# Graph attention on one Trainium2 core: q kept as three bf16 parts, spread over edges with bf16 one-hots

## The chip, the cores and the metric

The kernel runs on one NeuronCore of a Trainium2 chip. The metric is the device time of one execution in microseconds (us). The kernel before has a median of 6509.19 us over 3 runs (6508.78 to 6512.75).

## The reference

A graph network over 3125 nodes and 100000 edges (sorted by destination). Four transformer layers with 8 heads of 16 come first, then one message-passing layer with a 64-wide message:

```python
def _transformer_conv(h, src, dst, ...):
    q = (h @ Wq.T + bq)[dst]; k = (h @ Wk.T + bk)[src]; v = (h @ Wv.T + bv)[src]   # 8 heads x 16
    alpha = jnp.sum(q * k, axis=-1) / sqrt(D_HEAD)
    ex = jnp.exp(alpha - segment_max(alpha, dst)[dst])
    a = ex / (segment_sum(ex, dst)[dst] + 1e-16)
    out = segment_sum(a[:, :, None] * v, dst)
    x_r = h @ Ws.T + bs
    beta = sigmoid(concat([out, x_r, out - x_r]) @ Wbeta.T)
    return beta * x_r + (1 - beta) * out
# L0: h = gelu(x @ Wi); 4 layers of h = layer_norm(conv(h) + h); h = ffn(h) + h; then h @ Wo
# L1: msg = silu([x[src], x[dst], rbf(dist)] @ mw1 + mb1) @ mw2; mean over dst; update MLP
```

## The kernel before, in words

Nodes lie in 25 blocks (NB) of 128 rows. Edges lie in tiles of 128, one tile per partition column; two tiles share one node block, and 16 tiles (CH) make a chunk. There are 52 chunks per layer. Each layer has two kinds of stage.

**Node stage.** DVE mixes and normalizes five blocks at a time (L1044 to L1082), PE and ACT do the feed-forward part, and then the projections of the next layer follow (L666 on PE, L995 to L1004 on DVE): for each of 5 groups of 5 blocks PE makes a 128x256 product (q and the skip term `x_r` side by side) and a 128x264 product (k and v), DVE adds the biases and writes them to `qs` and `kvst`, and SP writes `kvst` to the table `kv_table` in HBM (L297). PE waits for these evictions by the semaphore `a_ev`, two banks deep. After the last group DVE clears `f_out` and `acc` (L1006, L1007).

**Edge stage.** POOL issues one indirect DMA per tile (L352): it gathers 128 rows of `kv_table` by the indices in `idx` into `slots`, a ring of 4 chunks. It starts when the table is written (`tab_out`), `acc` is cleared (`acc_zero`) and SP has loaded `idx` (L280), and goes on as slots come free (`slot_free`, set by PE at L561). For every group of 4 tiles, DVE compares `iota` with the destinations to make float32 one-hots `oh` (L847), PE turns them (L536), ACT copies the turned ones from PSUM to `ohT` (L377), and PE multiplies `ohT` by the block's rows of `qs` (L545): that product spreads q over edges. DVE multiplies it with the gathered keys (L865) and sums over heads (L871). The scores are turned at L569, scans along edges follow (L887 to L926), then exp on ACT, the weighting of v (L945), the sums over edges on PE with `oh` as weights (L559), and the addition to `acc` (L855). The work on chunk g is interleaved with the front of chunk g+1 in an order written out by hand (`attend_step` on PE, ACT and DVE). The message layer has the same form: `src_table` in place of `kv_table`, one further product with the distance basis (L549), an addition (L962) and silu (L442) in place of the attention.

All operands of these products are float32. In the trace a float32 product is two LDWEIGHTS and two MATMUL records.

## Time and profile before

| | |
|---|---|
| median of 3 runs | 6509.19 us |
| span of the profiled execution | 8606.0 us; no time beside the span is recorded for it |
| PE / PEld / DVE / ACT / POOL busy | 4926.9 / 4250.3 / 4108.2 / 1473.0 / 4188.6 us |
| mean granted TensorE clock | 0.699 of full speed |
| edge stages of the 4 attention layers (POOL's first gather to the first node instruction) | 233 to 1779, 1926 to 3487, 3639 to 5194, 5346 to 6907 us |
| edge stage of the message layer | 7108 to 8457 us |

The profiled execution is 2097 us longer than the median of the runs, so its waits are not simply those of a run that isn't profiled; durations of single instructions and waits have to be read apart. PE is TensorE's matmul stream, PEld its weight loads, DVE VectorE, ACT ScalarE, POOL GpSimd, SP SyncE.

### The profile page before, as it was taken

How to read it: one execution, taken by the hardware profiler on the slowest of the kernel's cores; microseconds unless marked ns; L12 is line 12 of the kernel's file. 1: busy time of each engine (PE TensorE's matmuls, PEld its weight loads, DVE VectorE, ACT ScalarE, POOL GpSimd, SP SyncE). 2: the span in 40 equal slices, each digit the busy share in tenths (PEclk: the TensorE clock that was granted, in tenths of full speed). 3: DMA queues.
4: the chain of work that ended last, by engine and by line, in shares of the span. 5: the costliest groups of instructions: out<-in, count | busy, mean ns of one | idle time of the engine just before them, and what ended most of it. 6: DMA issues, size and time to landing. Idle time of an engine off the chain costs nothing.

```text
span 8606.0 us, 101311 instructions
## 1 busy us (share of the span) xinstructions
PE 4926.9 (57%) x27346; PEld 4250.3 (49%) x27347; DVE 4108.2 (48%) x10183; ACT 1473.0 (17%) x3017; POOL 4188.6 (49%) x4185
## 2 busy tenths in 40 slices
PE   2465555664565555646556566456555664666664
PEld 1355454553454445535545455445455544565664
DVE  4455555564555555645555555455555552222224
ACT  1011111120111111211111112011111132333332
POOL 0555555506555555055555541555555406666660
PEclk9666666686666666866666668666666677887876
DMA  3322222313222223132222231222222201111111
GB/s 54 89 75 78 72 73 72 74 31 85 73 71 72 75 75 71 32 80 73 74 74 76 75 65 39 79 74 75 75 74 72 61 9 48 47 47 48 46 47 9
DMA packets 278744, 545.85 MB, mean 63 GB/s; under 512 B 128939, under 2 KB 155947, under 8 KB 278652
## 3 DMA queue, kind: packets, MB, share of 16 engines
q0 software_dynamic: 187040, 506.01, 23.1%
q1 hardware_dynamic: 84540, 31.89, 1.8%
q10 hardware_dynamic: 7072, 6.82, 0.2%
q8 instruction: 46, 0.75, 0.0%
q14 instruction: 46, 0.38, 0.0%
HBM read 525.19 MB, written 17.11 MB: 63 GB/s over the span
## 4 chain that ended last, share of the span: by engine, by line
another core or an unknown queue 43%; PE 27%; issue 15%; DVE 9%; ACT 3%; DVEq 1%; ACTq 1%; DMA 0%; SPq 0%; POOL 0%; POOLq 0%
PE bank L545 8%; PE bank L536 5%; PE bank L559 3%; PE bank L549 2%; DVE acc L855 1%; PE bank L697 1%; PE bank L689 1%; DVE oh L847 1%; PE bank L601 1%; PE bank L581 1%; PE bank L519 1%; DVE slots L962 1%; PE bank L527 1%; PE bank L668 1%
## 5 line engine op out<-in xcount | busy, mean ns | idle before, releaser
L352 POOL DMA_INDIRECT slots<-kv_table,idx x3328 | 3343.6, 1005 | 3434.2 <-PE bank L559 1621.0
L545 PE MATMUL bank<-qs,ohT 128*128 x8320 | 1766.8, 363 | 903.3 <-ACT ohT L377 438.9
L545 PEld LDWEIGHTS bank<-qs,ohT 128*128 128x128 f32 x8320 | 1550.0, 269 | 1021.8 <-issue 1002.9
L559 PE MATMUL bank<-slots,oh 128*128 128x136 f32 (+1 forms) x8320 | 1234.1, 299 | 167.2 <-issue 105.1
L559 PEld LDWEIGHTS bank<-slots,oh 128*128 128x128 f32 x8320 | 1133.0, 208 | 225.1 <-issue 127.5
L352 POOL DMA_INDIRECT slots<-src_table,idx x832 | 824.8, 991 | 735.4 <-issue 501.5
L855 DVE TENSOR_TENSOR acc<-acc,bank 128x136 f32 (+1 forms) x2080 | 605.2, 291 | 1022.5 <-remote 572.5
L536 PE MATMUL bank<-ident,oh 128*128 128x128 f32 x4160 | 1008.2, 390 | 108.3 <-DVE oh L847 64.2
L377 ACT COPY ohT<-bank 128x512 f32<-128x512 f32 x1040 | 601.7, 583 | 2055.9 <-remote 1167.0
L865 DVE TENSOR_TENSOR slots<-slots,bank 128x512 f32<-128x512 f32 x832 | 567.8, 682 | 630.9 <-remote 515.8
L536 PEld LDWEIGHTS bank<-ident,oh 128*128 128x128 f32 x4160 | 748.0, 210 | 202.6 <-issue 199.2
L847 DVE TENSOR_TENSOR oh<-iota,rel_e 128x1024 f32<-128x1024 f32 x520 | 630.7, 1214 | 0.5 <-issue 0.2
L945 DVE TENSOR_TENSOR slots<-slots,bank 128x544 f32<-128x544 f32 x832 | 542.2, 714 | 129.8 <-remote 115.7
L924 DVE TENSOR_TENSOR_SCAN fwd<-resets,icol,bank 128x128 f32<-128x128 f32 (+1 forms) x208 | 99.8, 480 | 1041.3 <-ACT icol L394 840.6
L871 DVE TENSOR_REDUCE alpha<-slots 128x32 f32<-128x512 f32 x832 | 566.5, 681 | 0.9
L581 PE MATMUL bank<-ident,fwd 128*1 128x128 f32 x208 | 66.3, 319 | 656.4 <-DVE bwd L889 308.0
L601 PE MATMUL bank<-ident,ex 128*128 128x128 f32 x208 | 94.8, 456 | 577.2 <-ACT ex L402 446.1
L962 DVE TENSOR_TENSOR slots<-slots,bank 128x512 f32<-128x512 f32 x208 | 141.4, 685 | 566.0 <-remote 333.4
L385 ACT COPY f_in<-bank 1x256 f32<-1x256 f32 x208 | 75.3, 362 | 1934.7 <-remote 1281.6
L588 PE MATMUL bank<-ones,c_row 1*128 1x1 f32 x416 | 119.5, 354 | 480.6 <-DVE c_row L914 257.4
L549 PE MATMUL bank<-resets 128*128 128x128 f32 x1664 | 370.1, 308 | 14.1 <-issue 13.9
L588 PEld LDWEIGHTS bank<-ones,c_row 1*128 1x128 f32 x416 | 101.8, 302 | 559.2 <-DVE c_row L914 305.2
(217 smaller groups left out, 4440.2 us busy)
## 6 DMA issues: line engine op xcount, KB each, us to landing
slots<-kv_table,idx POOLq DMA_INDIRECT x3328
slots<-src_table,idx POOLq DMA_INDIRECT x832
kv_table<-slots SPq DMA_DIRECT2D x20, 660.0 KB, 3.4
resets<-flat_len ACTq DMA_DIRECT2D x52, 128.0 KB
idx<-src_e SPq DMA_DIRECT2D x260, 8.0 KB
w<-in_w SPq DMA_DIRECT2D x8, 256.0 KB, 3.0
resets<-flat_rst SPq DMA_DIRECT2D x8, 208.0 KB, 10.6
slots<-flat_rst SPq DMA_DIRECT2D x8, 208.0 KB, 9.9
```

What stands on the lines that cost most here:

```text
L352: pool.indirect_dma_start(slots[:, k, t, 0:width], None, table, bass.IndirectOffsetOnAxis(ap=idx[:, k, t:t + 1], axis=0))\
L377: act.copy(ohT[:, j % 2, :, :].rearrange("p a b -> p (a b)"), bank[j % 2][:, :]).then_inc(oh_copied, 1)
L536: mm = pe.transpose(bank[j % 2][:, t * P:(t + 1) * P], oh[:, k % 2, j * G + t, :], ident[:, :])
L545: mm = pe.matmul(o, ohT[:, j % 2, t, :], qs[:, blocks[(j * G + t) // 2], 0:HID], start=True, stop=basis is None)
L549: mm = pe.matmul(o, rbf[:, k % 2, half, :], m_1c[:, q, :], start=False, stop=True)
L559: mm = pe.matmul(bank[6 + j % 2][:, o:o + width], oh[:, k % 2, t, :], slots[:, k, t, HID:HID + width], start=(t % 2 == 0), stop=(t % 2 == 1))
L847: dve.tensor_tensor(oh[:, k % 2, half * H:(half + 1) * H, :], bc(iota[:, :], H), bcl(rel_e[:, bass.ds(c * CH + half * H, H)], P), ALU.is_e ...
L855: dve.tensor_tensor(a_s, a_s, bank[6 + s // 2 % 2][:, o:o + width], ALU.add).then_inc(acc_done, 1)
L865: dve.tensor_tensor(keys, keys, bank[2 + j % 2][:, :].rearrange("p (t k) -> p t k", t=G), ALU.mult).then_inc(spread_used, 1)
L871: dve.tensor_reduce(alpha[:, :, j * G:(j + 1) * G].rearrange("p h t -> p t h"), slots[:, k, j * G:(j + 1) * G, 0:HID].rearrange("p t (h d) ...
L945: dve.tensor_tensor(vals, vals, bcl(exs[:, j * G:(j + 1) * G, :], VW), ALU.mult).then_inc(w_done, 1)
L962: dve.tensor_tensor(slots[:, k, j * G:(j + 1) * G, HID:2 * HID], slots[:, k, j * G:(j + 1) * G, 0:HID], bank[2 + j % 2][:, :].rearrange("p ...
```

## The change

`qs` (q and x_r side by side, float32) is replaced by `xr` (float32) and `q3`, which holds q as three bf16 tensors: q rounded to bf16, the rest rounded to bf16, and the rest of that. `ohT` becomes bf16 (ACT's copy L377 writes it so). The spreading product L545 becomes three products with the same `ohT` that add up in PSUM. DVE makes the parts in a new function after each group of five blocks, with four instructions that wait for each other. PSUM evictions of q and x_r are two instructions in place of one, so `a_ev` counts 3 per block in the attention layers.

```diff
-        qs = sb("qs", [P, NB, QS])
+        xr = sb("xr", [P, NB, HID])
+        q3 = sb("q3", [P, NB, 3, HID], BF16)
-        ohT = sb("ohT", [P, 2, G, P])
+        ohT = sb("ohT", [P, 2, G, P], BF16)
+        qf, qr = o_all[:, 0:BW, :], o_all[:, BW:2 * BW, :]
...
-                    mm = pe.matmul(o, ohT[:, j % 2, t, :], qs[:, blocks[(j * G + t) // 2], 0:HID],
-                                   start=True, stop=basis is None)
+                    for part in range(3):
+                        mm = pe.matmul(o, ohT[:, j % 2, t, :], q3[:, blocks[(j * G + t) // 2], part, :],
+                                       start=part == 0, stop=basis is None and part == 2)
...
+            def split_rows(i, nth, evicted):
+
+                def part(m):
+                    return q3[:, bass.ds(i * BW, BW), m, :]
+
+                dve.wait_ge(a_ev, evicted)
+                dve.tensor_copy(part(0), qf).then_inc(q_parts, 1)
+                dve.wait_ge(q_parts, START + 4 * nth + 1)
+                dve.tensor_tensor(qr, qf, part(0), ALU.subtract).then_inc(q_parts, 1)
+                dve.wait_ge(q_parts, START + 4 * nth + 2)
+                dve.tensor_copy(part(1), qr).then_inc(q_parts, 1)
+                dve.wait_ge(q_parts, START + 4 * nth + 3)
+                dve.tensor_tensor(part(2), qr, part(1), ALU.subtract).then_inc(q_parts, 1)
+                dve.wait_ge(q_parts, START + 4 * nth + 4)
...
-                        dve.tensor_tensor(qs[:, i * BW + b, :], bank[2 + b % 2][:, 0:QS], vec_qskv[:, 0:QS],
+                        dve.tensor_tensor(qf[:, b, :], bank[2 + b % 2][:, 0:HID], vec_qskv[:, 0:HID],
+                                          ALU.add).then_inc(a_ev, 1)
+                        dve.tensor_tensor(xr[:, bass.ds(i * BW + b, 1), :].rearrange("p a k -> p (a k)"),
+                                          bank[2 + b % 2][:, HID:QS], vec_qskv[:, HID:QS],
                                           ALU.add).then_inc(a_ev, 1)
...
+                    split_rows(i, ga, START + 3 * BW * (ga + 1))
```

In the message layer q's place is taken by the destination's part of the message input (L1110), which goes to `qf` and through `split_rows` in the same way.

## Rows read from the trace of the kernel before

**Rows 1.** Groups of instructions: POOL's gathers (busy us, mean ns, idle before and its releasers).
```profile
L352 POOL DMA_INDIRECT slots<-kv_table,idx x3328 | 3343.6, 1005 | 3434.2 <-PE bank L559 1621.0 <-issue 969.3 <-DMA idx<-src_e 789.3
L352 POOL DMA_INDIRECT slots<-src_table,idx x832 | 824.8, 991 | 735.4 <-issue 501.5 <-remote 164.2 <-DMA idx<-src_e 51.6
```

**Rows 2.** Timeline: first gathers of three layers, the first layer's end, the last gather.
```profile
233.34 0.94 POOL L352 DMA_INDIRECT slots<-kv_table,idx  x1 [167.31 <-DMA idx<-src_e]
...
1721.38 0.94 POOL L352 DMA_INDIRECT slots<-kv_table,idx  x1 [0.30 <-issue]
...
1779.15 0.29 DVE L1027 TENSOR_TENSOR slots<-vec 128x128 f32<-128x128 f32 x1
...
1925.92 0.94 POOL L352 DMA_INDIRECT slots<-kv_table,idx  x1 [203.59 <-DMA idx<-src_e]
1927.17 0.95 POOL L352 DMA_INDIRECT slots<-kv_table,idx  x1 [0.30 <-issue]
...
7108.52 1.11 POOL L352 DMA_INDIRECT slots<-src_table,idx  x1 [264.64 <-issue]
...
8403.14 0.95 POOL L352 DMA_INDIRECT slots<-src_table,idx  x1 [0.30 <-issue]
```

**Rows 3.** Timeline, once per chunk: after a layer's last gather, amid gathers, the message layer's end.
```profile
1746.08 0.33 PE L569 MATMUL bank<-ident,alpha 128*128 128x128 f32 x1 [0.21 <-DVE alpha L871]
...
1763.07 0.33 PE L569 MATMUL bank<-ident,alpha 128*128 128x128 f32 x1 [0.21 <-DVE alpha L871]
...
2498.66 0.33 PE L569 MATMUL bank<-ident,alpha 128*128 128x128 f32 x1 [0.21 <-DVE alpha L871]
...
2528.70 0.33 PE L569 MATMUL bank<-ident,alpha 128*128 128x128 f32 x1 [0.21 <-DVE alpha L871]
...
8423.38 0.68 DVE L962 TENSOR_TENSOR slots<-slots,bank 128x512 f32<-128x512 f32 x1
...
8437.82 0.68 DVE L962 TENSOR_TENSOR slots<-slots,bank 128x512 f32<-128x512 f32 x1
```

**Rows 4.** Waits: who waited for whom, us in total, times, longest.
```profile
ACT f_in L385 <- remote: 1281.6, 95, 19.0
```

**Rows 5.** Timeline, PEld: q's product for four tiles, at either clock.
```profile
2520.80 1.83 PEld L545 LDWEIGHTS bank<-qs,ohT 128*128 128x128 f32 x8
...
2525.16 0.98 PEld L545 LDWEIGHTS bank<-qs,ohT 128*128 128x128 f32 x8
```

**Rows 6.** Timeline of the projections, layer 1, last two groups of five blocks.
```profile
1906.85 0.43 DVE L1000 TENSOR_TENSOR qs<-bank,vec_qskv 128x256 f32 x1 [1.80 <-PE bank L668]
...
1910.97 0.43 DVE L1003 TENSOR_TENSOR slots<-bank,vec_qskv 128x264 f32 x1
...
1913.21 0.43 DVE L1000 TENSOR_TENSOR qs<-bank,vec_qskv 128x256 f32 x1 [1.80 <-PE bank L668]
...
1918.67 2.89 DVE L1007 MEMSET acc<- 128x3400 f32 x1 [0.66 <-issue]
```

**Rows 7.** Groups of instructions by form, DVE: five forms of the node stages.
```profile
L1110 DVE TENSOR_TENSOR qs<-bank,vec 128x128 f32 x25 | 7.3, 292 | 27.9 <-PE bank L708 27.9
...
L1059 DVE TENSOR_TENSOR slots<-slots,st 128x640 f32<-128x640 f32 x20 | 16.5, 826 | 0.7
...
L1158 DVE COPY slots<-slots 128x640 f32<-128x640 f32 x5 | 2.5, 493 | 0.6
...
L1103 DVE TENSOR_SCALAR xn<-slots 128x320 f32 x5 | 2.4, 486 | 0.2
...
L1105 DVE COPY slots<-slots 128x320 f32<-128x320 f32 x5 | 1.8, 358 | 0.7
```

**Rows 8.** Timeline of the message layer's projections, DVE: between groups, and the end.
```profile
7033.79 0.42 DVE L1097 TENSOR_TENSOR slots<-bank,vec 128x256 f32<-128x256 f32 x1 [3.96 <-PE bank L527]
...
7100.68 0.28 DVE L1112 TENSOR_SCALAR slots<-bank 128x128 f32 x1
...
7103.84 0.11 DVE L1115 MEMSET slots<- 128x64 f32 x1 [2.88 <-DMA src_table<-slots]
```

More of the change, by code:

```diff
@@ L201, in build_program @@
         slot_free = [sems(f"slot_free{k}_", NG) for k in range(RING)]
+        q_parts = sem("q_parts")
         oh_made, oh_turned, oh_copied, q_spread = sem("oh_made"), sem("oh_turned"), sem("oh_copied"), sem("q_spread")
@@ L216, in build_program @@
         out_ready, out_sent = sem("out_ready"), sem("out_sent")
-        counted = [sums_ready, deviations_ready, h_kept, a_ev, a_ps, acc_done, acc_scaled, acc_zero, act_ans, act_req,
+        counted = [q_parts, sums_ready, deviations_ready, h_kept, a_ev, a_ps, acc_done, acc_scaled, acc_zero, act_ans, act_req,
                    alpha_done, alpha_turned, arg_done, b_done, bwd_one, bwd_two, carries_packed,
@@ L295, in _ @@
                 with sp.Fori(0, NI) as i:
-                    sp.wait_ge(a_ev, START + 2 * BW * (l * NI + i + 1))
+                    sp.wait_ge(a_ev, START + 3 * BW * (l * NI + i + 1))
                     sp.dma_start(kv_table[bass.ds(i * BW * P, BW * P), :].rearrange("(b p) k -> p b k", p=P),
@@ L305, in _ @@
             with sp.Fori(0, NI) as i:
-                sp.wait_ge(a_ev, START + 2 * BW * (L * NI + i + 1))
+                sp.wait_ge(a_ev, START + 3 * BW * L * NI + 2 * BW * (i + 1))
                 sp.dma_start(src_table[bass.ds(i * BW * P, BW * P), :].rearrange("(b p) k -> p b k", p=P),
@@ L666, in _ @@
                     for b in range(BW):
-                        pe.wait_ge(a_ev, START + 2 * BW * (l * NI + i) + max(2 * b - 2, 0))
+                        pe.wait_ge(a_ev, START + 3 * BW * (l * NI + i) + max(3 * b - 3, 0))
                         pe.matmul(bank[2 + b % 2][:, 0:QS], hT[:, b * P:(b + 1) * P], w_qs[:, :], start=True, stop=True)\
@@ L706, in _ @@
                 for b in range(BW):
-                    pe.wait_ge(a_ev, START + 2 * BW * (L * NI + i) + max(2 * b - 2, 0))
+                    pe.wait_ge(a_ev, START + 3 * BW * L * NI + 2 * BW * i + max(2 * b - 2, 0))
                     pe.matmul(bank[4 + b % 2][:, 0:2 * HID], hT[0:64, b * P:(b + 1) * P], m_1[:, :], start=True, stop=True)\
@@ L1004, in _ @@
                                           ALU.add).then_inc(a_ev, 1)
-                dve.wait_ge(a_ev, START + 2 * BW * NI * (l + 1))
+                    split_rows(i, ga, START + 3 * BW * (ga + 1))
+                dve.wait_ge(a_ev, START + 3 * BW * NI * (l + 1))
                 dve.memset(f_out[:, :, :], -BIG).then_inc(node_done, 1)
@@ L1037, in _ @@
                 for b in range(NB):
-                    ins = dve.scalar_tensor_tensor(out=junk[:, NB + b, :], in0=qs[:, b, HID:2 * HID], scalar=1.0, in1=w12,
+                    ins = dve.scalar_tensor_tensor(out=junk[:, NB + b, :], in0=xr[:, b, :], scalar=1.0, in1=w12,
                                                    op0=ALU.mult, op1=ALU.mult, accum_out=logit[:, 1, b:b + 1])
@@ L1048, in mix_and_norm @@
                     dve.wait_ge(t_in, START + NI + 2 * NI * l + NI + i)
-                    step(dve.tensor_tensor(dx, qs[:, bs, HID:2 * HID], o_all[:, bs, :], ALU.subtract))
+                    step(dve.tensor_tensor(dx, xr[:, bs, :], o_all[:, bs, :], ALU.subtract))
                     dve.wait_ge(deviations_ready, START + r)
@@ L1109, in _ @@
                     dve.wait_ge(a_ps, START + 2 * BW * L * NI + BW * i + b + 1)
-                    dve.tensor_tensor(qs[:, i * BW + b, 0:HID], bank[4 + b % 2][:, HID:2 * HID],
+                    dve.tensor_tensor(qf[:, b, :], bank[4 + b % 2][:, HID:2 * HID],
                                       vec1[:, VEC1["mb1"]:VEC1["mb1"] + HID], ALU.add).then_inc(a_ev, 1)
                     dve.tensor_scalar(kvst[:, i * BW + b, 0:HID], bank[4 + b % 2][:, 0:HID], 0.0, None, ALU.add).then_inc(a_ev, 1)
+                split_rows(i, L * NI + i, START + 3 * BW * L * NI + 2 * BW * (i + 1))
             dve.wait_ge(tab_out, 16 * NI * (L + 1))
-            dve.wait_ge(a_ev, START + 2 * BW * NI * (L + 1))
+            dve.wait_ge(a_ev, START + 3 * BW * L * NI + 2 * BW * NI)
             dve.memset(slots[:, :, :, 2 * HID:2 * HID + 1], 1.0).then_inc(one_set, 1)
```

## The prediction, made before the change was run

> **What bounds the kernel now.** I read the busy times first, then the groups of instructions, the waits, and last the timeline at three places: amid the edge stages, after each layer's last gather, and in the projections. The first thing to see is that the profiled execution can't be read at face value: its span is 8606.0 us, the runs take 6509.19. So I look for the one resource that explains 6509.
>
> POOL issues 4160 gathers. One takes 1005 ns in the attention layers and 991 in the message layer, 3343.6 + 824.8 = 4168.4 us in all [rows 1], and the next starts 0.30 us behind it [rows 2]: 4168.4 + 4160 x 0.30 = 5416 us. With the 0.95 us that most gathers take (1927.17 - 1925.92 = 1.25 a gather), it is 5200. Outside these stretches POOL waits for node work: 233.3 us ahead of the first gather [rows 2]; 789.3 - 167.3 = 622.0 for the next three layers' indices [rows 1, 2], 203.6 the first of them; 264.6 ahead of the message layer; and 8606.0 - 8403.14 - 0.95 = 202 behind the last gather [rows 2]: 1322 us. In the profile POOL is far ahead at the end of each stretch: 1779.15 - 1722.32 = 57 us lie between the last gather and the first node instruction [rows 2]. Where gathers set the pace only about one chunk is left, some 20 us, which takes some 35 us from each of five: 1322 - 175 = 1147. Together 6347 to 6563 us, around the measured 6509.
>
> The other engines' chain alone doesn't reach that. Once a layer's gathers are over, a chunk with all its work takes 1763.07 - 1746.08 = 17.0 us, and 8437.82 - 8423.38 = 14.4 in the message layer [rows 3]. 208 x 17.0 + 52 x 14.4 + 1147 = 5432, over 1000 us short. Amid gathers the profile shows 2528.70 - 2498.66 = 30.0 us a chunk [rows 3], which 260 times over can't be what happens in 6509 us either. These 30 us are filled with waits whose releaser isn't found (1281.6 us for L385 alone [rows 4]), and POOL's 1621.0 us for PE's L559 [rows 1] follow from them. I take them for the cost of profiling. Then POOL's pace is 16 x 1.25 to 16 x 1.31 = 20.0 to 20.9 us a chunk against 17.0 for the others: **the gathers bound the edge stages, and everything else there has some 3 us of slack a chunk.** Between them the node stages lie bare.
>
> **The product.** 16 tiles a chunk with two float32 records each; four tiles take 1.83 us at 1.2 GHz and 0.98 at 2.4 [rows 5], 0.23 or 0.12 a record. Afterwards there are three bf16 products a tile. No row shows one. Below: half a record, as it goes through once where float32 takes two passes; then 3 halves against 2, 16 x 0.5 x 0.23 = 1.8 us a chunk less at 1.2 GHz, 1.0 at 2.4. Above: a whole record; then 3 against 2, 16 x 0.23 = 3.7 us more. I take the half, since a 128-column record is long enough to be streaming. In the forecast either is worth 0 us, for it lies under POOL's gathers: 17.0 + 3.7 = 20.7 still is no more than 20.9. Were the cover gone, it would be worth -1.8 to +3.7 us on each of 260 chunks. ACT's copy to bf16 reads the same 512 float32 columns from PSUM and stays at its price; the sums L559 still use the float32 `oh`.
>
> The Trainium skill (TensorE: Matmul & The Clock Gate, Back-to-back issue gap) gives N / 1.2 ns at the low clock and N / 2.4 + 2.5 at the high one, 107 and 56 ns for these 128 columns, and says under Weight-path perf modes that weights other than fp32 load faster. By that the saving would be 16 x (0.46 - 0.32) = 2.2 us a chunk at 1.2 GHz, and the case of the whole record falls; the sum above stays.
>
> **Evictions.** A 128x256 addition (L1000) gives way to two of 128x128, of 0.29 us each with some 0.21 from start to start (L1110's price) [rows 7], against 0.36: +0.06 a block, 0.3 us a group of five.
>
> **The split.** Four DVE instructions of 128x640, each waiting for the last. A two-input one costs 0.83 us (L1059). A copy costs 0.49 where both sides are contiguous (L1158); but here the source is contiguous and the target lies in 5 pieces of 128, 384 apart. Rows bound that: a 128x320 instruction between a contiguous and a 5-piece side took 486 ns (L1103), one with 5 pieces on both sides 358 (L1105) [rows 7]. So layout, not only type, decides, and I take the slow rate, 0.83; 0.49 stays as the lower bound. With 0.04 for each handoff the split is 4 x 0.87 = 3.5 us (lower bound 2.8), and about 0.1 more to wait for the last eviction.
>
> The Trainium skill (VectorE: DVE Perf Modes, What auto-detection actually checks) says that a one-source instruction takes its double rate if the outermost dims of source and target are both even or equal. A merged 640 against 5 is neither. By that the copies cost 0.83, by L1158's row alone 0.49, which is 10 to 15 us in the total.
>
> **What of it is bare.** Before, a group takes 1913.21 - 1906.85 = 6.36 us: 4.55 from the first eviction to the end of the last (1910.97 + 0.43), and 1.80 in which DVE waits for PE's turned and multiplied next group [rows 6]. The split comes at the head of this wait. PE goes on meanwhile, for its next two blocks need banks that are already free, so the evictions then find two blocks ready and take an estimated 4.1 us in place of 4.55; the loop's turn, some 0.3, is no longer hidden. New group: 4.1 + 0.3 (double evictions) + 0.1 + 3.5 + 0.3 = 8.3 at most, 8.0 if the doubled evictions overlap with PE's products as I expect: +1.65. Four transitions a layer: 6.6, and 0.35 for the first group: 7.0 us by which the last `kvst` goes out later, and with it SP's table write, the projections' loads and the indices behind them in SP's queue, which POOL waits for [rows 2]. The split after the last group is itself hidden: it delays only the clearing of `acc`, which ended at 1918.67 + 2.89 = 1921.56 while POOL started at 1925.92 [rows 2, 6]; 3.6 later leaves 0.8 for POOL to start in, so +0.3 as an estimate. Four layers: 4 x 7.3 = 29 us.
>
> In the message layer the split falls into DVE's wait of 3.96 us between groups; at the end it stands beside the 2.88 us wait for `src_table` [rows 8]: 3.6 + 7100.96 - 7103.84 = +0.7 us. The mix reads `xr` in place of a slice of `qs` at the same 640 columns: 0. Nothing new waits on SP or POOL.
>
> **Sum** against the profiled execution's own node stages: -0 + 29 + 0.7 = 29.9, of which I take 28, since evictions may overlap a little better than counted. These stages have no gathers and no unexplained waits, so I carry it over to the runs unchanged: 6509 + 28 = 6537 us. Bounds: with fast copies the group rises by 0.95 to 1.0, 4 x 4.3 = 17 us, 6526; with PE at 1.2 GHz in the longer gaps, about 1 us a group more, 4 x 4 = 16, 6553.
>
> **Rivals.**
>
> *The other engines set the pace after all* (faster). If their chain amid gathers takes just over POOL's pace without profiling too, PE's 1.0 to 1.8 us come off it until POOL's floor of 20.0 us is reached. For: 6347 as lower count leaves 162 us of room above POOL's floor; the profile does show POOL waiting for L559 [rows 1]. Against: 17.0 us a chunk once gathers end [rows 3]. It decides from a chain above POOL's own pace. The runs have (6509 - 1147) / 260 = 20.6 us a chunk, the floor is 20.0, and some gathers are stretched anyway, so 0.45 of it can go: 260 x 0.45 = 117 less, 28 more: 6420 us.
>
> *The split is all but hidden* (no change). Fast copies, a cheaper subtraction with a bf16 side, and evictions that catch up: 2 us a group in place of 3.6, against a wait of 1.80. For: the 1.80. Against: each instruction waits for the one ahead. Left 0.5 us a group, 4 x 2 = 8: 6517.
>
> *A bf16 product costs a whole record* (slower). Then PE has 3.7 us a chunk more, and with a lower granted clock, as PE's waits grow, the chain comes to 21.5 us against POOL's 20.9: 260 x 0.6 = 156, and 28: 6693. It decides from +3.9 us a chunk.
>
> **How the numbers follow.** The forecast 0.70, the faster rival 0.13, the hidden split 0.12, the slower one 0.05. A measurement of this kernel tells 0.2%, 13 us, from no change. Of the forecast's own range, 6522 to 6560, hardly any lies within that: slower 0.66 + 0.05 = 0.71, same 0.04 + 0.12 = 0.16, faster 0.13. The range leaves out the slower rival and the far part of the faster one: 6480 to 6565.
>
> **What would show it.** In the changed profile: gathers still 1.0 us with 0.30 between them; L545's group with 12480 MATMUL records, each about half as long; chunks after the last gather at 15 to 17 us; DVE's split at 3.5 us a group, with no wait for PE behind it; groups of 8 us in the projections; POOL's gaps between the attention layers 7 us longer, those before the message layer the same. It is wrong if the time falls by more than 13 us (the gathers weren't the bound), or if POOL's gaps grow and the time doesn't.

## The result, and the profile after

The changed kernel takes 6576.63 us (median of 4 runs, 6567.16 to 6587.76), the kernel before 6508.98 (4 runs): a ratio of 1.0101, 95% interval 1.0086 to 1.0117, or **+68 us**. I had forecast +28 (6537, range 6480 to 6565). On another chip, beside 15 runs of the kernel before, the ratio was 1.0104 (1.0088 to 1.0119). Slower was right, and mainly by the mechanism of the forecast; its size was off by 40 us, 12 us beyond the range.

One thing must be known to read what follows. The profile of before that I predicted from was not inflated by profiling. This kernel has two regimes: on three chips of this study the kernel before had a median of 6512 to 6532 us, on two others of 8262 and 8694, with all its runs there within 1.2% of it, profiled or not. (The runs on one chip were all made on one occasion, so it isn't shown that the chip decides and not something else of that occasion.) By its span of 8606.0 the trace of [rows 1 to 8] is one of the second kind. So the kernel before was profiled again, and the trace with a span of 6514.6 us (run e5_before_third, called its second profile below) is the one to compare with.

The page of the changed kernel: the chain that ended last, and its costliest groups.

```profile
POOL 58%; issue 24%; PE 8%; DVE 6%; POOLq 2%; DMA 1%; ACT 1%; SPq 0%; DVEq 0%; ACTq 0%
...
L355 POOL DMA_INDIRECT slots<-kv_table,idx x3328 | 3291.1, 989 | 1763.9 <-issue 1763.9
L549 PE MATMUL bank<-q,ohT 128*128 x12480 | 1272.4, 258 | 299.0 <-ACT resets L424 269.5
L549 PEld LDWEIGHTS bank<-q,ohT 128*128 128x128 bf16 x12480 | 1105.1, 120 | 379.5 <-issue 312.7
```

POOL's gathers fill the chain (58%), and between the gathers of a stage POOL waits for nobody. That is so in the second profile of the kernel before as well: the waits of [rows 1] for PE belong to the other regime, and the change didn't remove them. The products have become cheaper, as forecast: a weight load takes 120 ns on the mean where the second profile of the kernel before has 241, a MATMUL record 258 where it has 326; the 12480 MATMUL records take 253 us less in all than its 8320. That gains nothing, since POOL doesn't wait for it.

The rest shows in POOL's first gather of each stage. First the kernel before (second profile), then the changed one; the number in brackets is how long POOL stood before it.

```profile
231.65 0.94 POOL L352 DMA_INDIRECT slots<-kv_table,idx  x1 [165.78 <-DMA idx<-src_e]
...
1483.64 0.94 POOL L352 DMA_INDIRECT slots<-kv_table,idx  x1 [174.01 <-DMA idx<-src_e]
...
2740.30 0.94 POOL L352 DMA_INDIRECT slots<-kv_table,idx  x1 [173.98 <-DMA idx<-src_e]
...
3992.47 0.94 POOL L352 DMA_INDIRECT slots<-kv_table,idx  x1 [172.21 <-DMA idx<-src_e]
...
5300.71 1.10 POOL L352 DMA_INDIRECT slots<-src_table,idx  x1 [228.59 <-issue]
```

```profile
248.78 1.02 POOL L355 DMA_INDIRECT slots<-kv_table,idx  x1 [182.40 <-issue]
...
1511.36 1.03 POOL L355 DMA_INDIRECT slots<-kv_table,idx  x1 [189.12 <-issue]
...
2778.60 1.03 POOL L355 DMA_INDIRECT slots<-kv_table,idx  x1 [191.66 <-issue]
...
4040.63 1.03 POOL L355 DMA_INDIRECT slots<-kv_table,idx  x1 [188.21 <-issue]
...
5352.13 1.11 POOL L355 DMA_INDIRECT slots<-src_table,idx  x1 [230.72 <-issue]
```

Stages without gathers: 231.65 + 174.01 + 173.98 + 172.21 + 228.59 = 980.4 us before, 248.78 + 189.12 + 191.66 + 188.21 + 230.72 = 1048.5 after: +68.1, as much as the whole measured loss. Each attention layer pays 15 to 18 us, where I had 7.3; the message layer pays 2.1 here and 0.4 in a second profile of the changed kernel (run e16_after_again), where I had 0.7. What follows the last gather is the same (166.2 and 166.9 us). The gather stages take 5368 us before and 5350 after, but 5374 in that second profile: they vary by some 20 us from run to run, so the first pair of spans differs by 51 us only and the second by 70, and that +68.1 meets the +68 of the medians to the microsecond is chance. The second profile has +65 in the stages without gathers.

Where it goes inside a layer is seen in the projections of layer 1. Timeline of VectorE, changed kernel, third group of five:

```profile
1475.45 0.82 DVE L1007 TENSOR_TENSOR q<-slots,q 128x640 f32 x1
1477.00 0.29 DVE L1019 TENSOR_TENSOR slots<-bank,vec_qskv 128x128 f32<-128x128 f32 x1 [0.73 <-DVE q L1007]
...
1479.22 0.29 DVE L1019 TENSOR_TENSOR slots<-bank,vec_qskv 128x128 f32<-128x128 f32 x1 [0.58 <-PE bank L672]
...
1480.22 0.43 DVE L1025 TENSOR_TENSOR slots<-bank,vec_qskv 128x264 f32 x1 [0.51 <-PE bank L674]
...
1482.50 0.43 DVE L1025 TENSOR_TENSOR slots<-bank,vec_qskv 128x264 f32 x1
1483.08 0.82 DVE L1001 CAST q<-slots 128x640 f32 x1
...
1487.40 0.29 DVE L1019 TENSOR_TENSOR slots<-bank,vec_qskv 128x128 f32<-128x128 f32 x1 [0.71 <-DVE q L1007]
```

The split takes 3.6 us (1483.08 to 1486.68), and 0.71 pass from its end to the next eviction, the loop's turn. The evictions of the kernel before follow each other without waiting for PE in its later groups, and so do those of the changed kernel in its second and fourth group; in this third one they wait for PE four times, in the fifth five times. Why, the windows tell: the groups of layer 1, cut at the first eviction of each; first three groups of the kernel before (second profile), then all five of the changed kernel. The columns are named by the first line.

```profile
core 0: us, PE busy (x) PEld busy (x) DVE busy (x) ACT busy (x) POOL busy (x), PEclk, DMA share, GB/s
1444.10:1452.11 8.01, 7.02 (x26) 5.48 (x26) 4.29 (x10) 1.38 (x3) 0.00 (x0) 0.79 0.14 53
1452.11:1458.47 6.36, 5.37 (x26) 4.16 (x25) 4.20 (x10) 1.38 (x3) 0.00 (x0) 1.00 0.30 108
1458.47:1464.82 6.35, 5.36 (x26) 4.16 (x25) 4.19 (x10) 1.38 (x3) 0.00 (x0) 1.00 0.31 108
```

```profile
1457.30:1468.00 10.70, 8.18 (x31) 6.13 (x30) 7.72 (x19) 1.38 (x3) 0.00 (x0) 0.85 0.22 83
1468.00:1477.00 9.00, 5.50 (x25) 4.16 (x25) 7.54 (x20) 1.38 (x3) 0.00 (x0) 1.00 0.22 75
1477.00:1487.40 10.40, 6.93 (x25) 5.32 (x25) 7.61 (x20) 1.38 (x3) 0.00 (x0) 0.84 0.19 65
1487.40:1496.35 8.95, 5.50 (x25) 4.16 (x25) 7.52 (x19) 0.75 (x2) 0.00 (x0) 1.00 0.22 76
1496.35:1511.36 15.01, 4.58 (x12) 3.38 (x12) 11.78 (x22) 0.00 (x0) 0.00 (x0) 0.67 0.32 83
```

Where the granted clock stays at 1.00 a group takes 8.95 to 9.00 us; where it falls (0.84), the same 25 records of PE take 6.93 us in place of 5.50 and the group 10.4. In each of the groups from the second on, those at 1.00 and those at 0.84, PE stands still for 2.5 us behind its first two blocks, since the third (block 2) needs a bank that VectorE empties only behind the split. Timeline of PE, third group (the stop in brackets; the same two records took 0.70 us in the second group):

```profile
1477.97 1.22 PE L672 MATMUL bank<-w_qs,slots 128*128 128x256 f32 x2 [2.49 <-DVE slots L1025]
```

Behind the last group the split and the clearing of `acc` come one after the other, and POOL now waits for that:

```profile
1507.42 2.89 DVE L1030 MEMSET acc<- 128x3400 f32 x1 [0.66 <-issue]
```

### The profile page after: what moved, and what is told of

Read it like the earlier page. It is cut to its first block, busy times and chain, and to the rows that moved or that the text cites. A ratio compares the mean times of both kernels' runs of the same rounds, so it can differ in the third digit from the quotient of the medians.

```text
span 6565.4 us, 114167 instructions
## 1 busy us (share of the span) xinstructions
PE 4335.9 (66%) x31506; PEld 3771.8 (57%) x31507; DVE 4207.7 (64%) x10383; ACT 1483.0 (23%) x3017; POOL 4104.4 (63%) x4185
## 4 chain that ended last, share of the span: by engine, by line
POOL 58%; issue 24%; PE 8%; DVE 6%; POOLq 2%; DMA 1%; ACT 1%; SPq 0%; DVEq 0%; ACTq 0%
POOL slots L355 58%; PE bank L701 2%; PE bank L693 2%; PE bank L530 1%; PE bank L522 1%; PE bank L672 1%; DMA slots<-kv_table,idx 1%; PE bank L702 1%; POOLq L352 1%; PE bank L674 1%; POOLq L353 0%; PE bank L563 0%; SPq L276 0%; DVE slots L755 0%; PE bank L712 0%
## 5 line engine op out<-in xcount | busy, mean ns | idle before, releaser
L355 POOL DMA_INDIRECT slots<-kv_table,idx x3328 | 3291.1, 989 | 1763.9 <-issue 1763.9
L549 PE MATMUL bank<-q,ohT 128*128 x12480 | 1272.4, 258 | 299.0 <-ACT resets L424 269.5
L549 PEld LDWEIGHTS bank<-q,ohT 128*128 128x128 bf16 x12480 | 1105.1, 120 | 379.5 <-issue 312.7
L563 PE MATMUL bank<-slots,oh 128*128 128x136 f32 (+1 forms) x8320 | 1146.1, 287 | 121.3 <-DVE acc L859 117.5
L563 PEld LDWEIGHTS bank<-slots,oh 128*128 128x128 f32 x8320 | 1026.8, 193 | 165.1 <-DVE acc L859 152.3
L380 ACT CAST ohT<-bank 128x512 bf16<-128x512 f32 x1040 | 600.8, 583 | 764.4 <-PE bank L539 764.4
L573 PE MATMUL bank<-ident,alpha 128*128 128x128 f32 x208 | 79.5, 382 | 684.6 <-DVE alpha L875 684.6
L553 PE MATMUL bank<-resets 128*128 128x128 f32 x1664 | 437.1, 350 | 0.0
L553 PEld LDWEIGHTS bank<-resets 128*128 128x128 f32 x1664 | 309.9, 232 | 0.0
L445 ACT ACTIVATE slots<-slots 128x512 f32<-128x512 f32 x208 | 131.1, 630 | 607.8 <-DVE slots L966 600.9
```

The costliest lines, as they stand in the source:

```text
L355: pool.indirect_dma_start(slots[:, k, t, 0:width], None, table, bass.IndirectOffsetOnAxis(ap=idx[:, k, t:t + 1], axis=0))\
L380: act.copy(ohT[:, j % 2, :, :].rearrange("p a b -> p (a b)"), bank[j % 2][:, :]).then_inc(oh_copied, 1)
L549: mm = pe.matmul(o, ohT[:, j % 2, t, :], q3[:, blocks[(j * G + t) // 2], part, :], start=part == 0, stop=basis is None and part == 2)
L553: mm = pe.matmul(o, rbf[:, k % 2, half, :], m_1c[:, q, :], start=False, stop=True)
L563: mm = pe.matmul(bank[6 + j % 2][:, o:o + width], oh[:, k % 2, t, :], slots[:, k, t, HID:HID + width], start=(t % 2 == 0), stop=(t % 2 == 1))
```

## Experiments

There are eighteen runs of twelve kernels, on five chips. The kernel before took 8261.8 us (median) on the first chip, 6515.9 on the second, 6531.7 on the third, 8694.0 on the fourth and 6512.2 on the fifth; each ratio is to the one of the same chip. "First eviction to first gather" is the stretch of an attention layer in which the change acts, "stages without gathers" the sum of all such stretches of a run with its head and its tail: 1146.6 us before, 1215.4 after.

### The kernel before, profiled again

No edit.

> The kernel before, unchanged, for a second profiled execution. The first one took 8606 us of span against a median of 6509. Theory A (the first profile was one odd execution): this one has a span near 6507 us, chunk periods of 20.0 to 20.8 us in the edge stages as in the profile after, and 39 to 40 us from the first projection eviction to the first gather. Theory B (taking the profile slows this kernel by a third): a span near 8600 us again.

> The kernel before, unchanged, once more. Twice its profile showed 8606 and 8247 us where its timed median elsewhere was 6509. If TensorE, VectorE and ScalarE run here without the common stops of several microseconds that those two traces show, then: a span of 6500 to 6515 us, chunk periods of 20.0 to 20.8 us, stretches between the last gather of a layer and the first of the next 12 to 13 us shorter than in the changed kernel (189 us). If the stops are there again: 8200 us or more.

First chip: 8248.7 us, the other runs there 8179 to 8314. Second chip: 6516.4 us in the profiled run, median of 15 runs 6515.9; chunks of 20.0 to 21.6 us, 38.3 to 39.4 us from first eviction to first gather, POOL's waits 15 to 18 us shorter than in the changed kernel. Neither theory had it whole: a profiled run takes as long as the others on its chip, and the long trace was no odd execution, but the way that the kernel ran on that chip. My "cost of profiling" was a wrong reading, and that it led to the right bound was partly luck: the change happened to be timed in the first regime. What carried it was the count of gathers, which owes nothing to that reading; the 1147 us that I had worked out for the stages without gathers are 1146.6 in this trace.

### The split alone

```diff
+                    split_rows(i, ga, START + 2 * BW * (ga + 1))   # on a constant block, into parts nobody reads
```

> The kernel before plus the split alone: q stays as it was, the spread products stay float32 in one pass each, and the four split instructions work after every projection group on a constant block of rows whose parts nobody reads. Theory A (the added time lies between the first eviction and the first gather of each layer): 20 groups x 3.3 to 3.6 us make +55 to +72 us, 6564 to 6581 us, nearly all of the +67.6 us of the change. Theory B (half or more of the added time comes from the edge stages, by the three products or the bf16 one-hots): at most +34 us, at most 6543 us.

> The kernel before plus the split alone, again. Where the kernel before takes 6509 us: theory A (the added time lies between the first eviction and the first gather of each layer) gives +55 to +72 us; theory B (half or more of it comes from the edge stages) at most +34 us. Where the kernel before takes over 8000 us, as in the run on record, +105 us within 45 again.

1.0127 (1.0072 to 1.0182) on the first chip; **1.0112 (1.0096 to 1.0127)**, +73 us, on the second. Stages without gathers 1210.0 us, +63. Within the intervals the split alone is the whole loss. Its later groups take 8.6 us at full clock and 10.2 to 10.3 below it.

### The bf16 products alone

```diff
+        q3 = sb("q3", [P, NB, HID], BF16)          # filled with 0.25 once
-        ohT = sb("ohT", [P, 2, G, P])
+        ohT = sb("ohT", [P, 2, G, P], BF16)
+                    for part in range(3):
+                        mm = pe.matmul(o, ohT[:, j % 2, t, :], q3[:, blocks[(j * G + t) // 2], :],
+                                       start=part == 0, stop=basis is None and part == 2)
```

> The kernel before plus the bf16 one-hots and the three bf16 products alone: the products read one constant bf16 block (q's values are left out of the spread), evictions are as before, no split. Theory A (the products lie beside the gathers and cost nothing): 6509 us within 13 us. Theory B (the edge stages hold half or more of the added time): +34 us or more, from 6543 us. A third outcome, a gain from the 0.5 ms that TensorE is busy less, would need chunks that TensorE sets: below 6496 us.

> The kernel before plus bf16 one-hots and three bf16 products on a constant block, again. Where the kernel before takes 6509 us: theory A, within 13 us of it; theory B, +34 us or more. Where the kernel before takes over 8000 us, as in the run on record, 166 us more again: there the chunks are set by what TensorE, ScalarE and VectorE do in turn, and 16 more products a ring chunk cost time.

**1.0005 (0.9996 to 1.0014)** on the second chip, 1.0201 (1.0156 to 1.0247) on the first. Where the gathers set the pace the products are worth nothing either way. On the first chip they cost 166 us, although their weight loads and MATMUL records are shorter there too (128 and 276 ns, where the kernel before has 265 and 358): a cover that holds on one chip isn't there on every chip. What makes them cost that was not settled.

### Parts stored flat

```diff
-        q3 = sb("q3", [P, NB, 3, HID], BF16)
+        q3 = sb("q3", [P, 3, NB, HID], BF16)
```

> The changed kernel with its three parts stored one behind the other over all blocks, so that each split instruction writes one contiguous run of 640 columns in place of five runs of 128 with gaps. Theory A1 (the copies run at the slow rate because of the gaps, my argument on record): the two copies fall from 0.82 to about 0.49 us, 20 x 0.66 = 13 us less than the changed kernel, about 6563 us. Theory A2 (the rate goes by the float32 source or the engine's state, not by the gaps): 6577 us within 4.

> The changed kernel with the three parts stored one behind the other over all blocks, again; its trace on the other chip shows 494 ns for the two copies, 820 in the changed kernel. Where the kernel before takes 6510 us: 25 splits x 0.65 us = 16 us less if the whole split lies on the way (5 less for the message stage, where it was hidden: 13 us), so a ratio of 1.008 to the kernel before; more than that if the shorter pause also keeps TensorE's clock up in some groups (each 1.5 us).

The two copies fall from 820 to 494 ns: the layout decides, as argued. The first copy, changed kernel and flat parts (third chip):

```profile
L1001 DVE CAST q<-slots 128x640 f32 x25 | 20.5, 820 | 3.7
```

```profile
L1001 DVE CAST q<-slots 128x640 f32 x25 | 12.4, 494 | 3.5
```

The Trainium skill (VectorE: DVE Perf Modes, What auto-detection actually checks) has that rule, and the trace agrees. Ratio 1.0285 (1.0239 to 1.0331) on the first chip; on the third **1.0074 (1.0061 to 1.0087)**, where the changed kernel has 1.0104: 20 us less, with an uncertainty of some 13, of which 13 to 16 are the copies. The traces say it more sharply: stages without gathers 1178.5 us against 1215.4 and 1210.4, and first eviction to first gather 47.6 to 47.8 us, against 53.9 to 56.9 in two traces of the changed kernel, 6 us or more less a layer for 5 x 0.65 = 3.3 us of copies. The rest is the clock: PE's stop is 1.9 us now, and the windows of the second and third group show 1.00.

```profile
1469.70:1478.00 8.30, 5.50 (x25) 4.16 (x25) 6.84 (x19) 1.38 (x3) 0.00 (x0) 1.00 0.23 81
1478.00:1486.30 8.30, 5.50 (x25) 4.16 (x25) 6.87 (x19) 1.38 (x3) 0.00 (x0) 1.00 0.23 81
```

### TensorE kept busy during the split

```diff
                             .then_inc(a_ps, 1)
+                        if b == 1:
+                            for _ in range(4):     # 2 in the second kernel
+                                pe.matmul(bank[7][:, :], ident[:, :], hT[:, 0:4 * P], start=True, stop=True)
```

> The changed kernel with four more float32 products of 512 columns (into a bank that nobody reads) in each projection group, where TensorE stands still for 2.5 us until the split is over. Theory A (the standing lets TensorE's granted clock fall, and at the low clock the next group's evictions wait for TensorE: 10.4 to 10.7 us a group in place of 8.95): the granted clock stays at 1.00 and every group but the first takes 8.95 us, last group 4.5 us in place of 5.65; 3 to 5 us a layer less, 2 us more in the first group, in all 5 to 15 us less than the changed kernel. Rival (the 10.4 us have another cause, or the products lie in the way): no period shorter, up to 11 us more.

> The changed kernel with two extra products of 512 columns in each projection group (1.7 us at the full clock, in a standing time of 2.5 us). Theory A (the clock falls because TensorE stands still, and costs 1.5 us a group where it has fallen): clock 1.00 from the second group on, periods of 8.95 us, last group 4.5 us; per layer 1.5 + 1.2 us and in some 1.5 more, against 1.7 to 3.4 us more in the first group: 0 to 8 us less than the changed kernel in all. Rival (the clock falls all the same, as 2.5 us less 1.7 is still a pause): periods of 10.4 us as before.

Here a group's length is from its first eviction to the next group's, the last one's to the start of its last eviction (5.5 to 5.7 us in the changed kernel). Four products (3.6 us, longer than the stop): clock 1.00, all later groups 9.62 to 9.65 us, the last 4.8, but 1.0121 (1.0107 to 1.0136) in all, where the changed kernel has 1.0104. So the clock came out as expected and the time did not: I had forecast 5 to 15 us less. Two: every later group of all four layers 8.95 to 8.99, the last 4.05 to 4.08. The windows of the second and third group:

```profile
1958.21:1967.20 8.99, 7.20 (x30) 4.92 (x29) 7.54 (x20) 1.38 (x3) 0.00 (x0) 1.00 0.22 75
1967.20:1976.16 8.96, 7.19 (x30) 4.92 (x29) 7.52 (x20) 1.38 (x3) 0.00 (x0) 1.00 0.22 75
```

So it is the stop that costs the clock, and the clock that makes a group 10.4 us. As a cure it is poor: the first group, which has no such stop to fill, pays 1 to 2 us, and a layer takes 52.2 to 53.4 us in place of 53.9 to 56.9. Its ratio of 1.021 (1.0190 to 1.0231) is from the fourth chip and says nothing of the first regime.

### `acc` cleared early

```diff
+                dve.memset(acc[:, :, :], 0.0).then_inc(node_done, 1)      # ahead of the projections
                 with dve.Fori(0, NI) as i:
...
-                dve.memset(f_out[:, :, :], -BIG).then_inc(node_done, 1)
-                dve.memset(acc[:, :, :], 0.0).then_inc(acc_zero, 1)
+                dve.memset(f_out[:, :, :], -BIG).then_inc(acc_zero, 1)
```

> The changed kernel with acc cleared ahead of each layer's projections instead of behind the last split (and f_out's clearing as what releases GpSimd). Theory A (behind the last split the clearing's 2.9 us is what the first gather waits for): 2 to 3 us less for each of 5 stages, 10 to 15 us less than the changed kernel, so a ratio to the kernel before of 1.008 in place of 1.0101. Rival (the 2.9 us come back at the start, before the first eviction, or the copy of the key and value table to memory ends as late): within 4 us of the changed kernel.

1.0094 (1.0079 to 1.0110), which doesn't tell 1.008 from the changed kernel's 1.0101. The trace does: the start of the last eviction to the first gather falls from 9.3 us to 7.9 to 8.3 and no further, 1.0 to 1.4 us a layer in place of the 2 to 3 that I expected. At 8.0 to 8.3 the indices are next, as before the change [rows 2].

### One late split

```diff
-                    split_rows(i, ga, START + 3 * BW * (ga + 1))
...
                 dve.memset(acc[:, :, :], 0.0).then_inc(acc_zero, 1)
+                split_all(l)              # the same four instructions, on 25 blocks of o_all
...
                 pool.wait_ge(acc_zero, START + l + 1)
+                if k > 1:
+                    pool.wait_ge(q_parts, START + 4 * (l + 1))
```

> The changed kernel with one split of all 25 blocks behind the clearing of acc, so behind what releases the first gather, in place of 25 splits of 5 blocks between the projection groups. The split then takes 4 x about 4 us = 16 us while GpSimd gathers the first chunk; only the gathers of the third and fourth chunk wait for it. Theory A (the split costs only because it stands on the way from the first eviction to the first gather, and because TensorE idles meanwhile): the way from first eviction to first gather is back to 40 to 42 us from 54, 6576 us falls by 50 to 60 us to a ratio of 1.001 to 1.003 to the kernel before. Rival (the late start of the first chunks is not made up, since the gathers have no slack for it): ratio 1.007 or more.

**1.0047 (1.0034 to 1.0060)**. The stretch is back to 38.0 to 39.4 us and the stages without gathers to 1147.6: that half of theory A holds. But 29 us stay. They lie in the first chunk of each stage, 26.2 to 27.7 us long in place of 20.0 to 21.2. The late start isn't it, for these are POOL's own gathers. Timeline of layer 1, VectorE and POOL:

```profile
1495.12 3.49 DVE L1004 TENSOR_TENSOR slots<-slots,q 128x3200 f32<-128x3200 f32 x1
1495.46 3.97 POOL L357 DMA_INDIRECT slots<-kv_table,idx  x1 [173.87 <-DMA idx<-src_e]
1498.64 3.49 DVE L1006 CAST q<-slots 128x3200 bf16<-128x3200 f32 x1
1499.73 0.95 POOL L357 DMA_INDIRECT slots<-kv_table,idx  x1 [0.30 <-issue]
...
1502.16 3.49 DVE L1008 TENSOR_TENSOR q<-slots,q 128x3200 bf16<-128x3200 f32 x1
1502.24 4.24 POOL L357 DMA_INDIRECT slots<-kv_table,idx  x1 [0.30 <-issue]
```

A gather that meets a subtraction of two SBUF tensors ends 0.82 us behind it (1499.43 against 1498.61; 1506.48 against 1505.65). Beside the cast of the same length gathers take 0.95. The kernel before has such gathers too. From its second profile, a one-hot instruction (two SBUF inputs) and the gather that meets it; the gather again ends 0.82 us behind it:

```profile
1508.04 1.21 DVE L847 TENSOR_TENSOR oh<-iota,rel_e 128x1024 f32<-128x1024 f32 x1
...
1508.65 1.42 POOL L352 DMA_INDIRECT slots<-kv_table,idx  x1 [0.30 <-issue]
```

### The late split with one-operand instructions

```diff
-                dve.tensor_tensor(o_all, o_all, part(0), ALU.subtract).then_inc(q_parts, 1)
+                dve.tensor_scalar(o_all, o_all, 0.001, None, ALU.subtract).then_inc(q_parts, 1)
...
-                dve.tensor_tensor(part(2), o_all, part(1), ALU.subtract).then_inc(q_parts, 1)
+                dve.tensor_scalar(part(2), o_all, 0.001, None, ALU.subtract).then_inc(q_parts, 1)
```

> The kernel with one late split of all 25 blocks, whose two subtractions of one tensor from another are replaced by the subtraction of a constant: the second and third part of q then hold other values than they should; the rest is computed. Theory A (a gather that meets a VectorE instruction with two operands in SBUF is held until that ends; one with a single operand holds none): all gathers of the first chunk take 0.95 to 1.04 us, the first chunk 20.0 us in place of 26.4, 5 x 6.3 = 31 us less than the late split: within 10 us of the kernel before. Rival (the gathers are held by VectorE's traffic as such, or by its wide writes): the first chunk at 24 us or more, and 1.003 or more.

> The late split with one-operand instructions in place of its two subtractions (the second and third part of q hold other values), again. Its first chunk took 22.2 us in place of 26.4 of the late split on record. Where the kernel before takes 6510 to 6530 us: theory A (a held gather is time lost, since nothing but the gathers sets the pace) gives 5 x 4.2 = 21 us less than the late split, ratio 1.001 to 1.002. Rival (the late split's 29 us are not the holds): 1.0045.

Fourth chip: 1.0165 (1.0144 to 1.0186), first chunks of 22.0 to 23.6 us. Fifth: **1.0013 (1.0004 to 1.0022)**, by the ratios 22 us less than the late split (18 by the medians, each over the kernel before on its own chip), for 5 x 4.2 us of gathers. The rival's 1.0045 is well outside the interval: a held gather is lost time. Theory A was too simple at one point: the fast one-operand instruction holds a gather too, the slow one doesn't.

```profile
1492.70 1.83 DVE L1004 TENSOR_SCALAR slots<-slots 128x3200 f32<-128x3200 f32 x1
1493.11 2.23 POOL L357 DMA_INDIRECT slots<-kv_table,idx  x1 [172.16 <-DMA idx<-src_e]
...
1498.08 3.49 DVE L1008 TENSOR_SCALAR q<-slots 128x3200 bf16<-128x3200 f32 x1
1498.15 0.95 POOL L357 DMA_INDIRECT slots<-kv_table,idx  x1 [0.30 <-issue]
```

### A version that beats both

```diff
# e12: index loads of a stage's first four chunks ahead of its projections; acc cleared as above
+                for k in range(RING):
+                    stage_indices(k, l, 0)
                 with sp.Fori(0, NI) as i:
...
-                with sp.Fori(0, TURNS) as i:
+                with sp.Fori(1, TURNS) as i:
# e15, e18: that, and the one-hots by columns
-                dve.tensor_tensor(oh[:, k % 2, half * H:(half + 1) * H, :], bc(iota[:, :], H),
-                                  bcl(rel_e[:, bass.ds(c * CH + half * H, H)], P), ALU.is_equal).then_inc(oh_made, 1)
+                for t in range(H):
+                    ins = dve.tensor_scalar(oh[:, k % 2, half * H + t, :], iota[:, :],
+                                            rel_e[:, bass.ds(c * CH + half * H + t, 1)], None, ALU.is_equal)
+                ins.then_inc(oh_made, 1)
```

> The kernel before with the first four index loads of each stage issued ahead of the projections in place of behind three weight loads, and acc cleared ahead of the projections. In the trace of before the first index load is issued 3 us behind the last table store and the first gather starts 8.0 to 8.4 us behind the last eviction. Theory: the first gather then waits for the table store alone, 5.0 to 5.5 us behind the last eviction, 3 us less in each of 5 stages: 15 us less than before, ratio 0.9977. Rival (the store lands as late as the indices, or the time comes back at the start): ratio 1.000.

> The kernel before with the index loads and acc's clearing early, and each half of the one-hots (one instruction that compares two SBUF operands of 1024 elements, 1.21 us) made by eight instructions of 128 columns that compare one SBUF operand with a scalar of each partition. Theory A (the two-operand instructions hold the gathers they meet): the attention chunks fall from 20.75 to 20.0 us: 208 x 0.75 = 156 us less, ratio about 0.975. Theory B (the gathers are held by something else, such as the index loads): 0.998 as with the early indices alone. A third outcome: the eight instructions take so much more of VectorE that it sets the pace, or hold the gathers as well: 1.00 or more.

> The kernel before with early indices and clearing, and the one-hots from one-operand instructions, again. Its attention gathers took 963 ns on the mean in place of 1004. Where the kernel before takes 6510 to 6530 us: theory A (the chunk is 16 gathers, whatever VectorE does besides): 3328 x 0.030 to 0.041 us = 100 to 136 us less, and 15 of the early indices: ratio 0.977 to 0.983. Theory C (the one-hots' 16 x 0.235 us in place of 2 x 1.21 us, 1.3 us a chunk more, push VectorE's chain of some 17 to 18 us a chunk past the gathers' 20): 0.998 or more.

Early indices: **0.9980 (0.9968 to 0.9992)**, 5.4 us from last eviction to first gather, 13.5 us less in the stages without gathers. With the one-hots by columns 1.0281 (1.0260 to 1.0303) on the fourth chip, and **0.9855 (0.9840 to 0.9870)**, 6419.1 us, on the fifth: 93 us less than the kernel before. Groups of the kernel before (second profile), then of this one:

```profile
L352 POOL DMA_INDIRECT slots<-kv_table,idx x3328 | 3307.7, 994 | 1698.5 <-issue 1012.6 <-DMA idx<-src_e 686.0
...
L847 DVE TENSOR_TENSOR oh<-iota,rel_e 128x1024 f32<-128x1024 f32 x520 | 630.6, 1214 | 0.5 <-issue 0.2
```

```profile
L356 POOL DMA_INDIRECT slots<-kv_table,idx x3328 | 3219.0, 967 | 1687.4 <-issue 1687.4
...
L852 DVE TENSOR_SCALAR oh<-iota,rel_e 128x128 f32<-128x128 f32 x4160 | 880.5, 295 | 0.2
```

VectorE works 250 us more on the one-hots, and the kernel is faster: its gathers take 967 ns in place of 994, 3328 x 0.027 = 90 us. Of the 93 us some 13 are the early indices' (0.9980 without the one-hots), so the one-hots are worth about 80. The 100 to 136 us that I expected of them, and the ratio of 0.977 to 0.983, were too much; the chunks still take 20.2 to 20.4 us, not 20.0.

### The changed kernel beside them

> The changed kernel, unchanged, beside the other two on one chip. Where the kernel before takes 6510 to 6530 us: 1.010 again, within 0.002. Where it takes over 8000 us: 1.03, as the variant with flat parts showed 1.0285 there and lies 13 to 20 us below this one.

1.0104 (1.0088 to 1.0119), as quoted at the top.

## Why the prediction was right in kind and wrong in size

**The bound, and the products at 0: right**, where the gathers set the pace (products alone 1.0005, POOL waits for nobody). The weight loads, from which [rows 5] took the price, are half as long, as taken (120 ns against 241); the MATMUL records only fell to 258 from 326, and the sum over a chunk is 1 us less. The rivals "other engines set the pace" and "a whole record" fell. On the first chip the products cost 2%, and there POOL does wait for PE, so the cover of the forecast doesn't hold in that regime; but neither rival has it right, for the first expects a gain and the second longer records. I had the rows for it in hand [rows 1, 3, 4] and explained them away.

**The split's own price: right.** 3.6 us against 3.5; slow copies because of the layout.

**The group, "8.0 if the doubled evictions overlap": the step that failed.** At full clock a group is 4.5 us of evictions, 0.15, 3.6 of split and 0.73 of loop turn, 8.98. Two terms were too small: the evictions don't catch up to "an estimated 4.1 us" (PE has two blocks ready and is then itself held by the banks until 2.5 us later), and the loop's turn is 0.7, not "some 0.3". +2.6 us a group in place of +1.65: over 16 transitions 42 us in place of 26. With the evictions' 4.5 for 4.1, the turn's 0.7 for 0.3 and 0.15 on the split and its wait the sum comes out.

**The clock, kept out of the sum as a bound: it was real.** I had written "with PE at 1.2 GHz in the longer gaps, about 1 us a group more", 16 us, and left it out of the 28. The periods above 8.97 us sum up to 15 us in the four layers of the profile, less 5 that the kernel before has in its first groups, and the last groups take 5.5 to 5.7 us in place of 4.1: together 10 + 6 = 16 us. The flat parts and the filler products show for the later groups that this goes as soon as the clock stays up; for the first groups, some 2.5 us of the 16, it is argued from the length of PE's records alone. That is as much again as the 42 - 26 = 16 us of the group: my bound of 6553 had it, the 6537 did not.

**"The split after the last group is itself hidden", +0.3: too small.** From the start of the last eviction to the first gather it went from 8.0 to 8.3 us to 9.3, as the clearing of `acc` behind the split became what POOL waits for: about 1.2 us, 4.7 in four layers. The layer from which I took the slack [rows 2, 6] had the most of it, and VectorE's wait for the end of the split (0.35 us) wasn't counted.

**Message layer: right in kind** (+2.1 and +0.4 in two profiles, against +0.7). Sum of the four layers' stretches: 42 + 16 + 4.7 = 62.7 us, 62.9 in the trace; with 2.1 and some 4 us between last gather and first eviction and behind the end, which the change doesn't touch, 69.

## What to carry to other kernels

Put serial work of one engine between two groups only after asking what the other engine does meanwhile: if it stands, count the stretch once for the work and once more for the clock with which it comes back. Beside indirect DMAs from GpSimd, look which VectorE instructions read two SBUF tensors, or one at the fast rate: each gather that meets one waits for its end, and a slower form of the same work can win. And when a profile is a third longer than the timed runs, it may be another regime and not the profiler: what that profile says of covers and waits need not hold where the kernel is timed.

## What the runs showed of the hardware that I had not expected

**Held gathers.** As above: 3.97 and 4.24 us for a gather of 0.95. The Trainium skill (Advanced Engine Details and Errata, GPSIMD Details) says that GpSimd shares a read and a write interface with VectorE and conflicts with instructions that have two SBUF inputs or run in a two-port mode. The traces agree on both: held beside two-input subtractions and beside the one-operand instruction at 1.83 us for 3200 columns, not beside casts and the one-operand instruction at 3.49.

**The clock falls in one stop of 2.5 us, or right behind it,** in some groups (PEclk 0.84 over the group) and not in others of the same form (1.00). With stops of 1.9 us (flat parts) it fell in none of the later groups on the third chip and in one of twelve on the first. What tells them apart was not settled. In the first group of the first layer the record says 1.00 while a block's product takes 1.06 us, as in the groups at 0.84, and not 0.59: there the record can't be relied on.

**Two regimes.** On the chips of 8262 and 8694 us, ScalarE's and VectorE's instructions take as long as elsewhere (the copy L377 583 ns in both), and gathers are issued at the same pace while the ring fills (20.0 us a chunk, the longest of the first three 21.2), but ScalarE, TensorE and VectorE stop together in the gather stages, for up to 9 us at a time and once a stage, some 50 to 60 us into it, for 21 to 22; many of these waits the trace puts down to no instruction (`remote`, `issue`). In the kernel before on the first chip all three stand for over 2 us at once 269 times there, 994 us in all; on the second chip 53 times, 127 us, never over 4. The 867 us between them are half of the 1732 us between the two spans. ScalarE in the first chunk, kernel before, on the first chip and on the second:

```profile
270.95 0.58 ACT L377 COPY ohT<-bank 128x512 f32<-128x512 f32 x1 [9.23 <-remote]
280.67 0.16 ACT L394 COPY icol<-bank 128x2 f32<-128x2 f32 x1 [9.13 <-issue]
291.18 0.58 ACT L377 COPY ohT<-bank 128x512 f32<-128x512 f32 x1 [10.35 <-remote]
```

```profile
261.40 0.16 ACT L394 COPY icol<-bank 128x2 f32<-128x2 f32 x1 [1.49 <-PE bank L589]
262.45 0.59 ACT L377 COPY ohT<-bank 128x512 f32<-128x512 f32 x1 [0.89 <-PE bank L536]
```

The stops are there in the gather stages only; the projections of the kernel before take the same time in both regimes (38.3 to 39.6 us a layer from first eviction to first gather). Their cause stays open: no experiment was aimed at it.
